# A post-LN attention + FFN layer on 8 cores: the second half's attention output interleaved with the stage before it, its transposes moved from TensorE to DMA

## What is computed

```python
def _L0_attn_ref(x, wq, wk, wv, wo):          # x (1, 16384, 1024)
    Q = einsum('bne,de->bnd', x, wq); K = ...wk; V = ...wv
    energy = einsum('bnd,bne->bde', K, V)      # (64, 64), over all tokens
    context = einsum('bnd,bde->bne', Q, energy) * sqrt(3/64)
    return einsum('bnd,ed->bne', context, wo)
def _L0_ffn_ref(x, ...):                       # _tlin(x, w, s) = (x @ w.T) * s
    h = silu(_tlin(x, w1_w, w1_s)) * _tlin(x, w2_w, w2_s)     # 1024 -> 4096
    h = gelu(_tlin(h, h1_w, h1_s), approximate=False)         # 4096 -> 4096
    h = gelu(_tlin(h, h2_w, h2_s), approximate=False)         # 4096 -> 4096
    return _tlin(h, w3_w, w3_s)                               # 4096 -> 1024
x = layernorm(x + attn(x)); x = layernorm(x + ffn(x))
```

## Time and profile before

| | |
|---|---|
| three timed runs | 3388.3, 3622.1, 3889.7 us (median 3622.14) |
| the profiled execution, its own time | 3384.9 us |
| its span on the slowest core (7) | 3383.2 us; the eight cores 3370.8 to 3383.2 us |
| mean granted TensorE clock, each die | 0.947 and 0.946 |
| busy share of the span | PE 84%, ACT 25%, DVE 7%, POOL 7% |
| DMA | 347 MB, mean 103 GB/s |
| chain that ended last | PE 76%, ACT 6%, DMA 4%, issue 3%, DVE 3% |

### The profile page before, as it was taken

One profiled execution on the slowest core, in us unless ns is written; L12 is line 12 of the kernel. 1 busy time (PEld: TensorE's weight loads), 2 busy tenths in 40 slices (PEclk: granted clock), 3 DMA queues, 4 the chain that ended last, 5 costly groups with the idle time before them and its releaser, 6 DMA issues.

```text
span 3383.2 us, 40446 instructions; the slowest of 8 cores (3370.8 to 3383.2 us)
## 1 busy us (share of the span) xinstructions
PE 2853.3 (84%) x16601; PEld 1444.7 (43%) x16601; DVE 237.0 (7%) x513; ACT 833.0 (25%) x950; POOL 243.4 (7%) x460
## 2 busy tenths in 40 slices
PE   5773688889999989999998829989999999999990
PEld 4661344444444444444444414434444444444440
DVE  1112111100000000000000032220000000000002
ACT  4553333322222222222222223320000000000012
POOL 2220011000000000000000000000000000000000
PEclk9885799999999999999999959999999999999995
DMA  8993455556665556666555523322222222222212
GB/s 110 141 142 96 103 107 109 111 106 125 125 125 121 123 107 124 125 125 125 121 122 107 124 100 106 106 94 75 75 75 75 75 75 75 75 75 75 75 56 93
DMA packets 89169, 347.15 MB, mean 103 GB/s; under 512 B 10904, under 2 KB 10976, under 8 KB 70560
## 3 DMA queue, kind: packets, MB, share of 16 engines
q0 software_dynamic: 64800, 218.73, 34.9%
q10 hardware_dynamic: 14976, 92.28, 6.6%
q1 hardware_dynamic: 9216, 33.56, 2.8%
HBM read 361.83 MB, written 109.05 MB: 139 GB/s over the span
## 4 chain that ended last, share of the span: by engine, by line
PE 76%; ACT 6%; DMA 4%; issue 3%; DVE 3%; SPq 0%; ACTq 0%; DVEq 0%; POOLq 0%
PE PA L604 30%; PE PB L604 29%; PE PT L566 4%; PE PA L506 3%; PE PA L514 3%; PE PB L514 3%; PE PB L506 3%; ACT WTB L579 2%; DMA X1R<-x 2%; ACT WTB L473 1%; DMA X1R<-x1s 1%; ACT TS L338 1%; DVE X1F L399 1%; DVE X1F L367 1%; DVE X1F L676 1%
## 5 line engine op out<-in xcount | busy, mean ns | idle before, releaser
L604 PE MATMUL PA<-HB,WTB 128*128 128x512 bf16 x2560 | 574.9, 383 | 43.8 <-ACT WTB L579 32.0
L604 PE MATMUL PB<-HB,WTB 128*128 128x512 bf16 x2560 | 567.2, 380 | 30.6 <-ACT WTB L579 30.6
L604 PE MATMUL PA<-GB,WTB 128*128 128x512 bf16 x2048 | 457.3, 382 | 31.2 <-ACT WTB L579 25.5
L604 PE MATMUL PB<-GB,WTB 128*128 128x512 bf16 x2048 | 452.4, 379 | 23.7 <-ACT WTB L579 23.7
L579 ACT COPY WTB<-PT 128x1024 bf16<-128x1024 bf16 x288 | 283.9, 1013 | 481.4 <-PE PT L566 470.9
L604 PEld LDWEIGHTS PA<-HB,WTB 128*128 128x128 bf16 x2560 | 249.3, 99 | 342.4 <-issue 60.2
L604 PEld LDWEIGHTS PB<-HB,WTB 128*128 128x128 bf16 x2560 | 248.1, 98 | 322.5 <-issue 35.8
L604 PEld LDWEIGHTS PA<-GB,WTB 128*128 128x128 bf16 x2048 | 198.9, 98 | 267.9 <-issue 40.4
L604 PEld LDWEIGHTS PB<-GB,WTB 128*128 128x128 bf16 x2048 | 198.0, 98 | 256.3 <-issue 26.0
L506 PE MATMUL PA<-X1T,WTB 128*128 128x512 bf16 x512 | 124.2, 386 | 68.4 <-ACT WTB L473 50.5
L566 PEld LDWEIGHTS PT<-IDB,WSB 128*128 128x128 bf16 x2304 | 146.6, 98 | 56.7 <-issue 6.5
(11 more groups left out here) (116 smaller groups left out, 1361.7 us busy)
## 6 DMA issues: line engine op xcount, KB each, us to landing
WSB<-h POOLq DMA_DIRECT2D x128, 512.0 KB, 6.6
XB<-x POOLq DMA_DIRECT2D x128, 256.0 KB, 5.8
h1t<-WTB ACTq DMA_DIRECT2D x32, 1024.0 KB, 8.6
h2t<-WTB ACTq DMA_DIRECT2D x32, 1024.0 KB, 8.6
WTB<-h1t POOLq DMA_DIRECT2D x32, 1024.0 KB, 5.1
WTB<-h2t POOLq DMA_DIRECT2D x32, 1024.0 KB, 5.1
WSB<-w POOLq DMA_DIRECT2D x64, 256.0 KB, 5.7
wt<-WTB ACTq DMA_DIRECT2D x32, 512.0 KB, 6.1
```

Of the source, the lines that this page charges most:

```text
L604: first=first, last=last, src_buf=src_buf: fi(t.matmul(PP[rp][:, g_i * 512:(g_i + 1) * 512], WTB[:, so * H + b * 1024 + j * 128: so * H + ...
```

## The change

`emit_b3(h)` becomes `make_b3s(h)`, which returns a function `step(tau)` for one tile.

- For half 0 the eight steps are emitted one after the other, as before. For half 1, step `oc` is emitted ahead of output chunk `oc` in the w3 stage of half 0, by a hook in `emit_big_stage`. The loop over halves is written out, and the barrier between the halves becomes a `light_handoff`.
- In half 1's steps the attention product goes in two halves of 512 columns through the PSUM tensor PM, since PA and PB hold the w3 stage's sums: matmul, DVE's add, matmul, DVE's add; a small DVE addition joins the two partial row sums.
- In both halves of the tokens the PE transposes (L426) and ACT copies (L432) are gone. DVE's bf16 tile is stored by SP to a new DRAM tensor `x1bs`. After steps 3 and 7 SP waits for the stores and then issues 8 DMA transposes (`dma_start_transpose`), each 512 tokens x 128 columns from `x1bs` into X1T, each after a wait until the one before has landed.
- Stage 1 waits on PE for the first group of transposes ahead of its first token group and for the second ahead of its second.
- `light_handoff` makes POOL wait for the cache stores (counters `w0` and `w1`) too.
- `emit_ln` writes its unused squares to FT rather than TS1.

```diff
         w('s', 'w0', C['w0'])
         w('s', 'w1', C['w1'])
         w('g', 't', pe_gate)
+        w('g', 'w0', C['w0'])
+        w('g', 'w1', C['w1'])
...
+    def make_b3s(h):
...
+        def step(tau):
             th = 8 * h + tau
             r = tau % 2
-            if tau < 8:
+            if tau >= 2:
+                w('y', 'v', addm[tau - 2])
+            else:
+                w('y', f'y{r}', ysnap[r])
+                w('y', 'v', vsnap)
+            em('y', lambda s_, th=th, r=r: s_.dma_start(
+                out=X1R[:, r * E:(r + 1) * E],
+                in_=x[th * 128:(th + 1) * 128, :]).then_inc(SYL[r], 16))
+            xdma[tau] = inc(f'y{r}', 16)
+            if h == 0:
                 if tau >= 2:
-                    w('y', 'v', addv[tau - 2])
-                em('y', lambda s_, th=th, r=r: s_.dma_start(
-                    out=X1R[:, r * E:(r + 1) * E],
-                    in_=x[th * 128:(th + 1) * 128, :]).then_inc(SYL[r], 16))
-                xdma[tau] = inc(f'y{r}', 16)
-                if tau >= 2:
-                    w('t', 'v', addv[tau - 2])
+                    w('t', 'v', addm[tau - 2])
...
+            else:
+                for g_i in range(2):
+                    if g_i == 0:
+                        if tau >= 1:
+                            w('t', 'v', addg[(tau - 1, 1)])
+                    else:
+                        w('t', 'v', addg[(tau, 0)])
+                    em('t', lambda t, th=th, g_i=g_i: t.matmul(
+                        PM[:, 0:512], CT[:, th * 128:(th + 1) * 128],
+                        WOT[:, g_i * 512:(g_i + 1) * 512],
+                        start=True, stop=True).then_inc(ST, 1))
+                    attn[(tau, g_i)] = inc('t')
+                    w('v', 't', attn[(tau, g_i)])
+                    if g_i == 0:
+                        w('v', f'y{r}', xdma[tau])
+                        if tau >= 2:
+                            w('v', f'z{r}', x1st[tau - 2])
+                        else:
+                            w('v', f'z{r}', zsnap[r])
+                    em('v', lambda v, r=r, g_i=g_i: v.scalar_tensor_tensor(
+                        X1F[:, r * E + g_i * 512: r * E + (g_i + 1) * 512],
+                        PM[:, 0:512], 1.0,
+                        X1R[:, r * E + g_i * 512: r * E + (g_i + 1) * 512],
+                        ALU.mult, ALU.add,
+                        accum_out=(NM if g_i == 0 else NMG)[:, r:r + 1]
+                    ).then_inc(SV, 1))
+                    addg[(tau, g_i)] = inc('v')
+                w('v', 'v', addg[(tau, 1)])
+                em('v', lambda v, r=r: v.tensor_add(
+                    NM[:, r:r + 1], NM[:, r:r + 1],
+                    NMG[:, r:r + 1]).then_inc(SV, 1))
+                addm[tau] = inc('v')
+            lnv = emit_ln(r, r, dump=FT)
+            w('y', 'v', lnv)
+            if tau >= 2:
+                w('y', f'z{r}', x1st[tau - 2])
+            else:
+                w('y', f'z{r}', zsnap[r])
+            em('y', lambda s_, th=th, r=r: s_.dma_start(
+                out=x1s[th * 128:(th + 1) * 128, :],
+                in_=X1F[:, r * E:(r + 1) * E]).then_inc(SYS[r], 16))
+            x1st[tau] = inc(f'z{r}', 16)
...
+            em('v', lambda v, r=r: v.tensor_copy(
+                X1B[:, r * E:(r + 1) * E],
+                X1F[:, r * E:(r + 1) * E]).then_inc(SV, 1))
+            conv[tau] = inc('v')
+            w('y', 'v', conv[tau])
+            if tau >= 2:
+                w('y', f'x{r}', xbst[tau - 2])
+            else:
+                w('y', f'x{r}', xsnap[r])
+            em('y', lambda s_, th=th, r=r: s_.dma_start(
+                out=x1bs[th * 128:(th + 1) * 128, :],
+                in_=X1B[:, r * E:(r + 1) * E]).then_inc(SXB[r], 16))
+            xbst[tau] = inc(f'x{r}', 16)
+            if tau in (3, 7):
+                grp = tau // 4
+                w('y', 'x0', xbst[tau - 1])
+                w('y', 'x1', xbst[tau])
+                w('y', 't', tsnap)
                 for c in range(EC):
-                    em('t', lambda t, rp=rp, c=c: fi(t.transpose(
-                        PT[rp][:, c * 128:(c + 1) * 128],
-                        X1B[:, rp * E + c * 128: rp * E + (c + 1) * 128],
-                        IDB[:]), c == EC - 1))
-                x1tp[tp] = inc('t')
-                w('s', 't', x1tp[tp])
-                em('s', lambda s, rp=rp, tp=tp: s.copy(
-                    X1T[:].rearrange("p (c sl tk) -> p c sl tk", c=EC, sl=8)[:, :, tp, :],
-                    PT[rp][:, 0:1024].rearrange("p (c tk) -> p c tk", c=EC)
-                ).then_inc(SS, 1))
-                x1te[tp] = inc('s')
-        return C['s']
-
-    def emit_stage1(h, hook=None):
+                    w('y', 'q0', C['q0'])
+                    em('y', lambda s_, h=h, grp=grp, c=c: s_.dma_start_transpose(
+                        X1T[:, c * 1024 + grp * 512: c * 1024 + grp * 512 + 512],
+                        x1bs[(8 * h + grp * 4) * 128: (8 * h + grp * 4) * 128 + 512,
+                             c * 128:(c + 1) * 128]).then_inc(SXT, 16))
+                    inc('q0', 16)
+                st["xtg"][grp] = C['q0']
+
+        return step, st
+
+    def emit_stage1(h, hook=None, x1te3=0, x1te7=0):
         wdma = {}; wtp = {}; wte = {}; wte_lo = {}; mmv = {}; sil = {}; hv = {}; cw = {}
         for oc in range(HC):
             if hook is not None:
@@ -494,6 +555,10 @@
             for g_i in range(2):
                 s_ = oc * 2 + g_i
                 rp = s_ % 2
+                if oc == 0:
+                    w('t', 'q0', x1te3 if g_i == 0 else x1te7)
+                elif oc == 1 and g_i == 1:
+                    w('t', 'q0', x1te7)
                 if g_i == 0:
                     if h == 0:
                         w('t', 's', wte_lo[oc])
@@ -531,9 +596,12 @@
...
-    def emit_big_stage(wsrc, scl, src_buf, dst_buf, nout, func, cache, h):
+    def emit_big_stage(wsrc, scl, src_buf, dst_buf, nout, func, cache, h,
+                       hook=None):
         wdma = {}; wtp = {}; wte = {}; mmv = {}; gel = {}; cw = {}; rdv = {}
         for oc in range(nout):
+            if hook is not None:
+                hook(oc)
...
-    for h in range(2):
-        pre_b3_gate = C['t']
-        emit_b3(h)
-        light_handoff(pre_b3_gate)
...
+    b30, b30st = make_b3s(0)
+    for tau in range(8):
+        b30(tau)
+    light_handoff(pre_b3_gate)
+    g1_ = emit_stage1(0, x1te3=b30st["xtg"][0], x1te7=b30st["xtg"][1])
+    light_handoff(g1_)
+    g2_ = emit_big_stage(h1, SCH1, HB, GB, HC, AF.Gelu, h1t, 0)
+    light_handoff(g2_)
+    g3_ = emit_big_stage(h2, SCH2, GB, HB, HC, AF.Gelu, h2t, 0)
+    light_handoff(g3_)
+    b31, b31st = make_b3s(1)
+    g4_ = emit_big_stage(w3, SC3, HB, GB, EC, AF.Copy, w3t, 0,
+                         hook=lambda oc: b31(oc))
+    light_handoff(g4_)
+    fstep0 = make_final_ln(0)
+    g1b = emit_stage1(1, hook=lambda oc: fstep0(oc // 4) if oc % 4 == 0 else None,
+                      x1te3=b31st["xtg"][0], x1te7=b31st["xtg"][1])
+    light_handoff(g1b)
+    g2b = emit_big_stage(h1, SCH1, HB, GB, HC, AF.Gelu, h1t, 1)
+    light_handoff(g2b)
+    g3b = emit_big_stage(h2, SCH2, GB, HB, HC, AF.Gelu, h2t, 1)
+    light_handoff(g3b)
+    emit_big_stage(w3, SC3, HB, GB, EC, AF.Copy, w3t, 1)
+    barrier()
     fstep1 = make_final_ln(1, two_buf=True)
     for tau in range(8):
         fstep1(tau)
```

More of the change, by code:

```diff
@@ L90, in build @@
     SYL = [EE(nc.semaphore("SYL0")), EE(nc.semaphore("SYL1"))]
+    SXB = [EE(nc.semaphore("SXB0")), EE(nc.semaphore("SXB1"))]
+    SXT = EE(nc.semaphore("SXT"))
     SYS = [EE(nc.semaphore("SYS0")), EE(nc.semaphore("SYS1"))]
@@ L155, in build @@
     QENG = {"l": "g", "g0": "g", "g1": "g", "g2": "g", "g3": "g",
+            "x0": "y", "x1": "y", "q0": "y",
             "y0": "y", "y1": "y",
@@ L371, in emit_ln @@
         return inc('v')
-    def emit_b3(h):
-        attn = {}; addv = {}; x1tp = {}; x1te = {}; xdma = {}; x1st = {}
-        for ti in range(OT // 2 + 1):
-            tau = ti
+    def make_b3s(h):
+        st = {"xtg": {}}
+        attn = {}; addm = {}; addg = {}; conv = {}; xdma = {}
+        x1st = {}; xbst = {}
+        ysnap = {0: C['y0'], 1: C['y1']}
+        zsnap = {0: C['z0'], 1: C['z1']}
+        xsnap = {0: C['x0'], 1: C['x1']}
+        vsnap = C['v']
+        tsnap = C['t']
+        def step(tau):
             th = 8 * h + tau
             r = tau % 2
-            if tau < 8:
-                if tau >= 2:
-                    w('y', 'v', addv[tau - 2])
-                em('y', lambda s_, th=th, r=r: s_.dma_start(
-                    out=X1R[:, r * E:(r + 1) * E],
-                    in_=x[th * 128:(th + 1) * 128, :]).then_inc(SYL[r], 16))
-                xdma[tau] = inc(f'y{r}', 16)
-                if tau >= 2:
-                    w('t', 'v', addv[tau - 2])
+            if tau >= 2:
[8 more added lines that the diff above has]
+            if h == 0:
+                if tau >= 2:
```

(20 more changed lines are left out.)

31 lines of the change are left out of this document (8 added, 23 removed), and 1 row of the table C.

## The result

The changed kernel takes 1.0126 times as long as the kernel before, with a 95% interval of 1.0108 to 1.0143: 43 us more on 3387 us, where the forecast was 92 us more. The profiled execution took 3432.1 us against 3384.9 us, +47 us. (Some executions of every 8-core program here are several per cent longer on all cores of a die at a lower granted clock; all ratios leave them out.)

The account below looks back on a forecast made before the run. Bound: `emit_b3` stretches with PE mostly idle behind a chain of x loads, VectorE and ScalarE. Terms +70, +3.5, +75.5 and −57 sum to +92 on 3384.9 us: 3477 us, range 3390 to 3580.

Parts of the forecast that it names:

- price list: Ahead of the sum: one 128 KB DMA transpose with wake-up takes 4.1 us in `b3(0)`, 5.0 in the w3 stage.
- as quick as plain loads: Rival on the DMA transposes: each takes 3.35 us like a plain load, sum +54, 3439 us; chance 0.27.
- Part 1: Half 0's `b3(0)`, hidden by nothing: later loads, two waits for transpose groups and a cold PE cost +70 us.
- T0: Length of a group of eight DMA transposes in half 0's `b3(0)`, taken as 33 us.
- Part 2: Handoffs in half 0: GpSimd's wait for cache stores delays the next weight loads, three times, +3.5 us together.
- Part 3: w3 stage of half 0: gaps and slower clock ahead of chunks, plus a stall for tile 4, +75.5 us.
- T1: Length of a group of eight DMA transposes in the w3 stage, taken as 40 us.
- Part 4: End of the overlap, last w3 matmul to stage 1's second chunk: 42.4 us instead of 99.5, −57.
- The overlap holds: Rival: transposes near a plain store's time, 1.95 us with wake-up, 3380 to 3394 us, not slower; chance 0.08.
- t: Landing time plus wake-up of one 128 KB DMA transpose in SP's queue; the forecast hung on it.
- Heavy: Rival: a transpose takes 6.7 us in half 0, 8.9 in the w3 stage, sum +196, 3581 us; chance 0.20.
- Far smaller pieces: Argument against transposes as fast as plain loads: their destination is written in far smaller pieces than any trace row shows.

## Why the prediction was right or wrong

- **The time, the size and the class were wrong.** 3477 us was forecast, 3432 measured in the profile; +2.7% against +1.3%; slower by over 2% had 0.63, and it came out within 2%, which had 0.34. The direction was right.
- **The step that failed is the price list**, "I take t0 = 4.1 us ... and t1 = 5.0 us". Measured, a transpose with its wake-up took 2.7 and 3.0 us in half 0 and 3.5 and 3.2 in the w3 stage. Four groups of eight multiply this one number by 32: 145.6 − 99.7 = 46 us, all of the miss. The row chosen, a weight load in 256-byte pieces, was issued by GpSimd, with a cast, as one of nine loads in a row; the nearer rows for a lone transfer of SP were the ones I used as lower bounds. And the reason for that row, "3.4 us in long rows and 4.0 us in 256-byte pieces", does not hold in the same list, where a third load of this size, in long rows too, stands with the highest of the four figures:

```profile
WQn<-wq POOLq DMA_DIRECT2D x1, 128.0 KB, 4.2
```

- **The rival "as quick as plain loads"** came nearest (+54); the mean with its wake-up, 3.1 us, was a little below even its 3.35.
- The Trainium skill, page "Advanced Engine Details and Errata", section "X-Bar Transpose (TRN2)", says that transposing DMAs are as fast as regular ones. By this rule the forecast would have been 3439 us, 7 from the profiled time; the trace agrees for these 128 KB transfers (2.6 us against an estimated 3.25 for a plain load), less so for 1 MB, where the transpose took 6.2 us at best, a plain load of GpSimd 5.1 (median of `WTB<-h1t`) and the undisturbed store of the earlier trace rows 4.3. The rival that goes by it had 0.27, the forecast 0.45.
- **The form of the sum was right.** With the measured groups it gives +46, and every run that changed the groups or the order moved the way that its terms say: −44 without waits in a group (expected −57), −47 without half 0's transposes (expected −47), +64 without the overlap (expected +54). That +46 meets the profiled +47 to 1 us is partly luck: by the marks the parts below are 3 to 5 us off, in both directions, and the marks add up to +40, the ratio to +43.
- **Part 1** (2·T0 + 4.5): 50 us with the measured groups, 47 by the marks and 47 by experiment.
- **Part 2** (+3.5): about 1.5 us, none of it seen in the marks. The load was late as forecast, but the copy behind it no longer waited for a slowed store; I had subtracted too little.
- **Part 3**: 4.0 us of gap a chunk was right to 0.1; the clock's part was 2.3 us (2.0 to 2.7 on the cores), not 1.7; the stall was 19.8 us where T1 − 7.5 gives 20.7. Together 64 with the measured group, 68 by the marks.
- **Part 4**: 99.5 down to 23 us, where T1 + 0.4 + 2 gives 28; −76 on the slowest core and −74 by the marks.
- **The other rivals.** "The overlap holds" needed t under 2 us, groups of 15.6, and forecast 3380 to 3394. The changed kernel never came near; without the waits three of its four groups did (12 to 16 us to the last landing), and the time, 3386, is the rival's. Its words "early enough for tile 4" do not fit its own numbers: T1 − 7.5 leaves a stall of 8 us, and 9.9 were seen. "Heavy" (54 and 71 us a group) was not seen in any run; the longest group, 39.9 us where chunk 4 ran beside it, is just the forecast's T1.
- **"Far smaller pieces"**, the argument against quick transposes, finds no support in the packets: the changed kernel moved 17664 more packets under 512 bytes than the kernel before, about 550 for each of the 32 transposes, and so about 240 bytes a packet (an estimate from the two counts, 28568 and 10904).

What stays open: why the same group is 3 us longer at the start of stage 1 than in the middle of `b3(0)`. It is one transfer, the first of the eight, that lands after 6.8 us (6.5 to 9.0 in the other runs with waits); only the neighbouring traffic was seen, no run took it away. The same holds for the slow transfers in the w3 stage.

## What to carry to other kernels

When a chain of transfers that wait for each other is put into a queue, its price is count times landing time, wherever a later instruction of that queue is wanted: find that instruction first, and price the single transfer from the lone transfers of the same queue, not from the row that shares its piece size. A stage that is hidden under another one must also be hidden in each engine's queue: ahead of a chunk's first copy the same step cost 6 us, behind its last copy 1. A queue that no longer waits is not yet free: with the waits taken out, the load behind the group landed 7 us later than a lone one. And before a stall is filled with another stage's work, look at whether the order of two DMAs in one queue makes it: the two such exchanges at the end gave 63 of the 137 us (3314 to 3251).

## What the runs showed of the hardware

- A DMA transpose of 512 x 128 bf16 occupies SP for 1.12 us, against 0.32 to 0.42 us for a plain 256 or 512 KB transfer where the queues are quiet (up to 1.2 us in the w3 stage), and lands after 2.4 us at best; one of 1 MB occupies SP for 4.2 us and lands after 6.2, both at best. The Trainium skill, page "DMA: Bandwidth & Descriptors", section "Latency and other measured facts", has 261 GB/s as the effective bandwidth of a transpose with a non-contiguous middle dimension and about 350 to 400 for the contiguous case. The slope here, 0.92 MB more in 3.8 us, is 240 GB/s, an estimate from two sizes and below both.
- Several transposes in flight from one queue help less than their issue times say: landing went from 2.6 to 4.1 us, SP's issue up to 2.6 us, and a group, counted to its last landing, from 23 to 29 us only to 12 to 16, and to 16 to 22 where the w3 stage's loads ran beside it.
- TensorE that had idled 3.64 us came back at 1.2 GHz at every such gap of the w3 stage: 16 matmuls took 5.4 to 6.2 us instead of 3.45. With 2.3 us of filler matmuls in the gap and 1.37 us of idling behind them it stayed at 2.4 GHz.
